# A two-round graph network on one core: the low part of a block of adj made in one subtraction or in two

## What is computed

```
x = layernorm(x + relu((adj @ x) @ kernel + bias))
u, v = x, v_node_feats
for _ in range(3):
    v = mlp(adj @ u, uv_W1, uv_b1, uv_W2, uv_b2, uv_W3, uv_b3)
    u = mlp(adj @ v, vu_W1, vu_b1, vu_W2, vu_b2, vu_W3, vu_b3)
out = layernorm(x + v)
```

## Time and profile before

| what | value |
|---|---|
| median of 3 runs | 1170.84 us |
| the profiled execution, its own time | 1170.68 us |
| its span, first to last instruction | 1168.8 us |
| TensorE busy | 1154.0 us, 99% |
| VectorE busy | 738.1 us, 63% |
| ScalarE busy | 660.9 us, 57% |
| DMA, mean rate | 224 GB/s |
| mean granted TensorE clock | 0.999 |

### The profile page before, as it was taken

The page is one execution under the profiler, slowest core; times in us unless marked ns, Lnnn a source line. Parts: engine busy times, 40 slices in busy tenths (PEclk is TensorE's granted clock), DMA queues, the critical chain, the costliest instruction groups (busy, mean ns, idle before and its releaser), DMA issues.

```text
span 1168.8 us, 13697 instructions
## 1 busy us (share of the span) xinstructions
PE 1154.0 (99%) x5236; PEld 953.2 (82%) x5236; DVE 738.1 (63%) x890; ACT 660.9 (57%) x809; POOL 0.2 (0%) x4
## 2 busy tenths in 40 slices
PE   7999999999999999999999999999999999999997
PEld 6888888888888888888888888888888888887776
DVE  7997676458564555555545746554566555678884
ACT  7765555346554555555444754554556444667874
POOL 0000000000000000000000000000000000000000
PEclk9999999999999999999999999999999999999999
DMA  9988785568366646555656736655665555589870
GB/s 383 406 302 321 247 271 191 206 215 288 125 205 210 216 161 224 189 184 180 216 180 216 250 116 223 207 179 178 207 225 184 195 200 214 188 296 362 297 261 36
DMA packets 72209, 261.60 MB, mean 224 GB/s; under 512 B 8016, under 2 KB 8656, under 8 KB 71120
## 3 DMA queue, kind: packets, MB, share of 16 engines
q1 hardware_dynamic: 72000, 260.61, 63.6%
q10 hardware_dynamic: 144, 0.13, 0.0%
HBM read 258.61 MB, written 2.10 MB: 223 GB/s over the span
## 4 chain that ended last, share of the span: by engine, by line
PE 93%; DMA 3%; DVE 2%; ACT 1%; issue 0%; SPq 0%; DVEq 0%; ACTq 0%
PE agg_ps L892 28%; PE agg_ps L885 28%; PE agg_ps L878 28%; PE pre_ps L789 4%; DMA adj_raw<-in_adj 3%; PE hid_ps L750 1%; PE hid_ps L752 1%; PE hid_ps L751 1%; DVE adj_lo L742 1%; ACT adj_hi L613 1%; PE hid_ps L811 1%; PE hid_ps L825 0%; ACT feat_hi L613 0%; DVE stats L626 0%; ACT resid L528 0%
## 5 line engine op out<-in xcount | busy, mean ns | idle before, releaser
L742 DVE TENSOR_TENSOR adj_lo<-adj_raw,adj_hi 128x1024 fp32r<-128x1024 f32 x464 | 548.1, 1221 | 226.4 <-ACT adj_hi L613 221.0
L878 PE MATMUL agg_ps<-adj_hi,feat_hi 128*128 128x512 f32 x1484 | 587.0, 396 | 7.5 <-ACT adj_hi L613 7.5
L885 PE MATMUL agg_ps<-adj_hi,feat_lo 128*128 128x512 f32 x1484 | 579.4, 390 | 0.0
L613 ACT ACTIVATE adj_hi<-adj_raw 128x1024 fp32r<-128x1024 f32 x464 | 468.3, 1052 | 86.0 <-PE agg_ps L892 72.4
L892 PE MATMUL agg_ps<-adj_lo,feat_hi 128*128 128x512 f32 x1484 | 458.8, 390 | 0.2 <-DVE adj_lo L742 0.2
L878 PEld LDWEIGHTS agg_ps<-adj_hi,feat_hi 128*128 128x128 f32 x1484 | 279.6, 188 | 66.4 <-issue 9.8
L885 PEld LDWEIGHTS agg_ps<-adj_hi,feat_lo 128*128 128x128 f32 x1484 | 279.5, 188 | 59.7 <-issue 2.4
L892 PEld LDWEIGHTS agg_ps<-adj_lo,feat_hi 128*128 128x128 f32 x1484 | 278.9, 188 | 59.6 <-DVE adj_lo L742 1.1
L507 ACT ACTIVATE hid<-hid_ps,params 128x512 f32<-128x512 f32 (+1 forms) x80 | 54.5, 681 | 61.0 <-PE hid_ps L752 50.6
L578 ACT ACTIVATE in_hi<-part 128x512 fp32r<-128x512 f32 x24 | 15.2, 634 | 110.4 <-DVE part L731 110.4
L507 ACT ACTIVATE post<-pre 128x512 f32<-128x512 f32 x39 | 24.6, 631 | 79.8 <-DVE pre L709 79.8
(11 more groups left out here) (78 smaller groups left out, 382.3 us busy)
## 6 DMA issues: line engine op xcount, KB each, us to landing
adj_raw<-in_adj SPq DMA_DIRECT2D x472, 512.0 KB, 5.6
adj_raw<-in_adj SPq DMA_DIRECT2D x8, 1024.0 KB, 8.1
resid<-in_x SPq DMA_DIRECT2D x8, 256.0 KB, 8.1
out<-resid SPq DMA_DIRECT2D x7, 256.0 KB, 5.5
params<-in_weights SPq DMA_DIRECT2D x1, 386.0 KB, 4.7
b_row<-in_bias_rows SPq DMA_DIRECT2D x1, 128.0 KB, 5.6
out<-resid ACTq DMA_DIRECT2D x1, 128.0 KB, 2.1
out<-resid SPq DMA_DIRECT2D x1, 128.0 KB, 2.2
```

The lines of the kernel that those rows point to most:

```text
L613: act.activation(split_hi(b)[:, i * CHUNK:(i + pieces) * CHUNK], adj_raw[:, h % RAW, 0:pieces * CHUNK], ACT.Copy).then_inc(adj_hi_ready, 1)
L742: dve.tensor_tensor(split_lo(b)[:, slot], adj_raw[:, h % RAW, 0:pieces * CHUNK], split_hi(b)[:, slot].bitcast(F32), ALU.subtract).then_inc ...
L878: pe.matmul(group_bank(g), feat_hi[feats][:, tile(src, i)], split_hi(b)[:, piece(i)], start=start, stop=False)
L885: pe.matmul(group_bank(g), feat_lo[feats][:, tile(src, i)], split_hi(b)[:, piece(i)], start=False, stop=False)
```

## The change

From the first block on whose first use is at place 24 or later in the order of uses (block 22, its halves 44 and 45), VectorE skips a block's first half. At the place of the second half it waits for the high part of both, and makes the low part of all 2048 columns in one instruction, which raises `adj_lo_ready` by 2. Blocks 0 to 21 are left as they were. This touches 222 of 244 blocks: 444 subtractions of 1024 columns become 222 of 2048. Nothing else is changed: the loads, the waits on other engines and the order of everything else stay.

```diff
+    def low_at_once(self, b):
+
+        return self.first_use(b) >= FIRST_ROWS * self.rows
...
+                    h += 1
+                    if plan.low_at_once(b):
+                        if i == 0:
+                            continue
+                        raw = adj_raw[:, (h - 2) % RAW:(h - 2) % RAW + 2, :].rearrange("p k f -> p (k f)")
+                        dve.wait_ge(adj_hi_ready, h)
+                        dve.tensor_tensor(split_lo(b), raw, split_hi(b).bitcast(F32), ALU.subtract)\
+                           .then_inc(adj_lo_ready, 2)
+                        continue
                     slot = slice(i * CHUNK, (i + pieces) * CHUNK)
-                    dve.wait_ge(adj_hi_ready, h + 1)
-                    dve.tensor_tensor(split_lo(b)[:, slot], adj_raw[:, h % RAW, 0:pieces * CHUNK],
+                    dve.wait_ge(adj_hi_ready, h)
+                    dve.tensor_tensor(split_lo(b)[:, slot], adj_raw[:, (h - 1) % RAW, 0:pieces * CHUNK],
                                       split_hi(b)[:, slot].bitcast(F32), ALU.subtract).then_inc(adj_lo_ready, 1)
-                    h += 1
```

## The result

| | kernel before | changed kernel |
|---|---|---|
| median of 6 runs | 1170.80 us | 1179.82 us |
| profiled execution, its own time | 1170.68 us | 1179.72 us |
| its span | 1168.8 us | 1177.9 us |
| TensorE busy | 1154.0 us | 1158.5 us |
| VectorE busy | 738.1 us | 722.9 us |

The ratio is 1.0077, with a 95% interval of 1.0066 to 1.0089. The forecast was 1175.6 us with a range of 1172.4 to 1178.3 us: the direction was right, the size 4.97 us where 9.0 us came, and the time lies outside the range.

A forecast was written before the change was run, and what follows sets the result against it. The prediction took TensorE to bound the kernel and added pauses of 0.30 + 1.26 + 0.55 + 0.35 + 0.60 + 1.07 + 0.84 = 4.97 us, giving 1175.6 us against 1170.84, with a range of 1172.4 to 1178.3 us.

The forecast's parts named there:

- What bounds the kernel: TensorE, busy for 972.00 of 972.00 us from 64 to 1036 us; VectorE's savings cannot shorten that stretch.
- The price of one instruction: A subtraction of 2048 columns takes 2.29 us (2.12 to 2.44); where VectorE waits for ScalarE, pairs end 1.07 us later.
- looked for reserves under some 1 us: Reading the timeline around every place where TensorE waits on VectorE, or on ScalarE behind it, for small reserves.
- Blocks 37 to 39: End of row 4 in sweep 0: late low parts make TensorE pause twice, 0.30 us together.
- The turns: Later `hid_lo` makes TensorE pause: 1.26 us at the turns to sweeps 2, 3 and 4, 0.55 at sweep 1.
- The last unit in parts: Near 1041 us, `hid_lo` comes later behind two long instructions: a TensorE pause of 0.35 us (0 to 0.65).
- The last sweep: From 1036 us: late steps on VectorE and ScalarE make TensorE pause for 0.60, 1.07 and 0.84 us.
- The place at 1092 and 1095 us: In the last sweep, one pause grows by 0.45 us and one shrinks as much: 0 (-1.0 to +0.5).
- VectorE full in the last sweep: Rival: VectorE's queue sets the last sweep's steps, so shorter work pays: 1169.3 us, chance 0.06.
- The last sweep gives its delays back: Rival: late steps there find gaps on other engines; only 2.46 us stay: 1173.1 us, chance 0.13.
- The raw ring: Rival: SyncE gets a pair's places back late, so loads come late; up to 2 us more: 1177.7 us, chance 0.09.

The follow-up runs named there:

- e3: Kernel before with the long subtraction for 167 blocks, leaving out the last sweep's blocks and 20 ahead of pauses: 1171.12 us, ratio 1.0005.
- e4: Changed kernel, but each long subtraction raises the semaphore by 1, with all waits counting accordingly: 1177.87 us, ratio 1.0061 to the kernel before.
- e5: Kernel before, still in halves, but each half raises the semaphore by 2 and all waits count double: 1171.28 us, ratio 1.0006.
- e2: Kernel before with the long subtraction for four blocks alone (72, 108, 144, 180): 1172.54 us, ratio 1.0016.
- e7: Changed kernel's order, but two subtractions of 1024 columns at the place of the second half: 1171.87 us, ratio 1.0010 to the kernel before.
- e1: Kernel before with the long subtraction only for the 36 blocks first used in the last sweep: 1174.04 us, ratio 1.0028.
- e6: Kernel before, but SyncE waits for both halves' low parts before loading into the place of either: 1170.60 us, ratio 1.0000.
- e9: Changed kernel with 2, or 48, more already met waits at the start of VectorE's program: 1180.23 and 1179.51 us, one execution each.

## Why the prediction was wrong

*What bounds the kernel* was right: TensorE, with no pause between 64 and 1036 us; VectorE's saved time brought nothing (e3: 167 long instructions, no gain).

*The price of one instruction* was right to 0.1%: 2289 ns against 2.29 us. The lateness worked out from it was not general. It holds where VectorE had waited for the second half too: 52 of the 141 long instructions that wait, and they end 1.14 us late against TensorE (median), the 1.07 worked out and 0.07 more, since raising the semaphore by 2 parts the wait from the instruction (e4, e5). In the 89 others VectorE had made the second half right behind the first; in 63 of them ScalarE's two roundings end 0.95 us apart, which is faster than VectorE's 1.135 us. The median lateness of the 89 is 0.66 us. I had read the increment in the diff and given it no price.

*The step that failed* is "looked for reserves under some 1 us" around the places where TensorE waits. I compared VectorE's last step with its consumer on TensorE, one step at a time, for `adj_lo`, `in_lo`, `hid_lo` and `part`, and put every other step at nothing. I did not follow the bias over ScalarE to `feat_lo`. Its reserve of 0.03 us (496.83 to 497.00, less the way of 0.14) can be read in the trace of before. It costs 1.88 us in the changed kernel, and e2 measures it alone with 1.9 us. Nor did I follow `part` over ScalarE's `in_hi` and its roundings to `hid_lo` near 519 us: its reserve of 1.07 us is more than the 0.95 us of the long instruction there, and less than the 1.22 us that came with ScalarE's 0.27. It cost 1.01 us over four places, which e3 and e7, with this pair or all pairs left in two, don't have. No run parts the 0.95 from the 0.27; they are read from the trace. These two terms, forecast at 0, are 2.89 of the 4.1 us that were missing.

*The terms that were there* held outside the last sweep, each a little small. Blocks 37 to 39: two pauses, as worked out, 0.52 for 0.30. The turns: 1.76 for 1.26, and 0.58 for 0.55. The last unit in parts: 0.74 for 0.35, with 0.35 us from the late start. What is missing in most is the 0.07 us and up to another 0.11 us: after a held matmul, the one behind it starts 0.31 to 0.34 us later (499.85 and 500.19 us at the first `feat_lo` shown), not 0.227.

*The last sweep*, 2.49 for 2.51 us, is in part luck. ScalarE's late queue was right: `std` waited 1.63 us, and `hid` comes late. But at 1112 and 1128 us TensorE already waited for VectorE's `part`, 0.25 and 0.76 us, which the prediction had at nothing; so less was left for `hid`. The place at 1092 and 1095 us gave 0.22 us back, where it was put at 0. Two slips of the working stand beside this: 1114.99 - 1114.43 with the way of 0.14 is 0.70 us, not 0.60 (the 0.60 would need the 0.05 us between ScalarE's end and TensorE's start that the trace shows, 1131.05 and 1131.10), and the lower bound of 1173.1 us leaves out the -1.0 of that place; with it, it is 1172.1.

*The rivals.* VectorE full in the last sweep: no, e1 is 2.5 us slower there. The last sweep gives its delays back: only at 1095 us. The raw ring: no (e6), apart from the 0.15 us or less in two other kernels' traces.

*The range* was built from the instruction's duration alone, and that was the best known of all numbers. It held no width for places that I hadn't found.

## What to carry to other kernels

In a kernel whose matrix engine never waits, a change on another engine can only cost, and what it costs is set by the few places with the smallest reserve: here 55 of 222 long instructions made all but half a microsecond of the 9 us, and four of them a fifth. To find them, don't pair each step with its direct consumer; follow every step that comes late through all engines until one has idle time of its own or TensorE is reached. Where the second input is still being made, merging two instructions moves the first half's work behind the wait; do it only where the reserve behind covers that, as it did for 167 of the 222 here. And where pauses are a matter of order, the order can be mended: five halves moved gave 1.65 us.

## What the runs showed of the hardware

- An increment of a semaphore by 2 in place of 1 makes the wait ahead of that instruction an instruction of its own: VectorE starts 0.10 us after the producer's end, not 0.03 us (174 of 174 starts in e5 against 175 of 175 in the kernel before). In e4 this was worth 1.8 us of the 9.
- A pause of TensorE costs 0.08 to 0.11 us more than the wait. In the changed kernel the held matmul at 478.64 us is followed 0.31 us later, the one at 499.85 us 0.34 us later, where unheld ones are 0.227 us apart:

```profile
478.95 0.39 PE L763 MATMUL hid_ps<-hid_lo,w_hi 128*128 128x512 f32 x1
```

- VectorE starts some 0.35 us late at instructions 63 above a multiple of 128 of its program, where that instruction had waited and its wait is an instruction of its own just ahead. Seen five times in three kernels (191, 703 and 959 in the kernel of e9 with 2 waits, 831 in the changed kernel and in e1); with the wait as part of the instruction, 831 in the kernel before starts in time. What happens there isn't shown by any run.
